# A transformer tower on one core: patch weights on four row groups, and the second item's first stages moved into the attention of the first

## Time and profile before

| | us |
|---|---|
| median of 3 runs | 4034.71 (4033.22 to 4037.4) |
| the profiled execution, its own time | 4041.78 |
| its span | 4040.0 |
| first score of the phase `first` starts | 120.93 |
| TensorE busy | 3811.9 (94%) |
| VectorE busy | 2886.2 (71%) |
| ScalarE busy | 2619.9 (65%) |
| GpSimd busy | 860.0 (21%) |

### The profile page before, as it was taken

One profiled execution on the slowest core, in us unless ns is written; L12 is line 12 of the kernel. 1 busy time (PEld: TensorE's weight loads), 2 busy tenths in 40 slices (PEclk: granted clock), 3 DMA queues, 4 the chain that ended last, 5 costly groups with the idle time before them and its releaser, 6 DMA issues.

```text
span 4040.0 us, 62363 instructions
## 1 busy us (share of the span) xinstructions
PE 3811.9 (94%) x21508; PEld 1330.2 (33%) x21508; DVE 2886.2 (71%) x4955; ACT 2619.9 (65%) x4768; POOL 860.0 (21%) x1263
## 2 busy tenths in 40 slices
PE   6988999999999999999999999999999999999896
PEld 3223333333333333333333333333333333333232
DVE  3866767778686777867678676777867677777672
ACT  0555767667676666767667676666767667676564
POOL 4122113122121322213122121312213122121211
PEclk7899999999999999999999999999999999999998
DMA  5203211222012122111222122122111222111100
GB/s 106 40 15 60 43 36 33 46 48 44 22 35 56 33 43 43 37 34 33 46 48 43 27 38 49 32 43 47 38 29 33 50 44 43 31 36 25 28 6 6
DMA packets 119067, 156.36 MB, mean 39 GB/s; under 512 B 24847, under 2 KB 66575, under 8 KB 118717
## 3 DMA queue, kind: packets, MB, share of 16 engines
q1 hardware_dynamic: 118753, 152.38, 19.0%
HBM read 120.01 MB, written 29.36 MB: 37 GB/s over the span
## 4 chain that ended last, share of the span: by engine, by line
PE 81%; ACT 8%; issue 4%; DVE 3%; SPq 2%; DMA 1%; POOL 1%; ACTq 0%; POOLq 0%; DVEq 0%
PE acc L911 23%; PE side_st L897 21%; PE nat L885 19%; PE side_st L854 3%; PE side_st L750 3%; PE side_st L727 2%; ACT prob L1101 2%; PE side_st L840 2%; ACT hidden L1073 2%; PE side_st L807 1%; DVE tile_max L1294 1%; ACT hidden L1019 1%; PE side_st L772 1%; SPq L525 1%; PE side_st L765 1%
## 5 line engine op out<-in xcount | busy, mean ns | idle before, releaser
L1294 DVE TENSOR_REDUCE tile_max<-nat 128x1 f32<-128x512 f32 x4096 | 2585.7, 684 | 1002.6 <-PE nat L885 972.0
L1101 ACT ACTIVATE prob<-side_st 128x512 f32<-128x512 f32 x4096 | 2205.8, 600 | 1271.7 <-PE side_st L897 1236.8
L897 PE MATMUL side_st<-q_rows,k_rows 99*128 99x512 bf16 x4096 | 1562.6, 384 | 45.9 <-ACT prob L1101 28.9
L885 PE MATMUL nat<-k_rows,q_rows 96*128 96x512 bf16 x4096 | 1532.2, 385 | 30.2 <-DVE tile_max L1294 24.0
L911 PE MATMUL acc<-prob,v_padded 128*32 128x512 f32 x8192 | 1096.1, 607 | 14.5 <-ACT prob L1101 13.5
L897 PEld LDWEIGHTS side_st<-q_rows,k_rows 99*128 99x128 bf16 x4096 | 398.6, 98 | 1213.9 <-ACT prob L1101 812.1
L885 PEld LDWEIGHTS nat<-k_rows,q_rows 96*128 96x128 bf16 x4096 | 400.8, 98 | 508.4 <-DVE tile_max L1294 276.1
L1455 POOL TENSOR_SCALAR max_parts<-neg_max 128x16 bf16<-128x16 f32 x128 | 26.5, 207 | 1868.4 <-DVE neg_max L1301 1868.3
L911 PEld LDWEIGHTS acc<-prob,v_padded 128*32 128x32 f32 x8192 | 162.3, 108 | 377.4 <-ACT prob L1101 216.0
L840 PE MATMUL side_st<-ln_rows,w 64*128 64x512 f32 x512 | 139.5, 622 | 28.7 <-ACT hidden L1073 23.2
L1380 POOL TENSOR_SCALAR ln_s<-ln_s 128x8 f32<-128x8 f32 x64 | 13.0, 203 | 676.8 <-DVE ln_s L1202 673.2
(11 more groups left out here) (124 smaller groups left out, 1994.5 us busy)
## 6 DMA issues: line engine op xcount, KB each, us to landing
q_rows<-q_scratch SPq DMA_DIRECT2D x576, 64.0 KB
k_rows<-k_scratch SPq DMA_DIRECT2D x192, 192.0 KB
x_rows<-in_x SPq DMA_DIRECT2D x62, 512.0 KB, 6.3
q_scratch<-hidden SPq DMA_DIRECT2D x32, 384.0 KB
k_scratch<-hidden SPq DMA_DIRECT2D x96, 128.0 KB
group_weights<-in_routed SPq DMA_DIRECT2D x64, 129.0 KB, 2.1
q_rows<-max_rows SPq DMA_DIRECT2D x512, 3.0 KB
out_h<-out_rows SPq DMA_DIRECT2D x16, 256.0 KB, 2.1
```

What stands on the lines that cost most here:

```text
L885: eng.matmul(NAT[use % len(NAT)][:, :], QA[u][0:K_NAT, h, c:c + P], KA[u][0:K_NAT, h, kh * 512:kh * 512 + 512], start=True, stop=True)\
L897: eng.matmul(RING[TILE_BANK[n0 + n]][:, :], KA[u][0:K_ALL, h, t * P:t * P + P], QA[u][0:K_ALL, h, half * 512:half * 512 + 512], start=True ...
L1101: eng.activation(prob[:, n % TILES, :], RING[TILE_BANK[n0 + n]][:, :], ACT.Exp).then_inc(exp_done, 1)
L1294: eng.tensor_reduce(mx[:, q % 2, j // 8, j % 8 // 2, j % 2:j % 2 + 1], NAT[use % len(NAT)][:, :], AX.X, ALU.max).then_inc(nat_free, 1)
```

## The change

The table `dft` is now loaded four times, to partitions 0, 32, 64 and 96, by DMAs that ScalarE issues. W is loaded in four quarters of 72 KB by SP to the same four places (`w_rows`), all in `prob`. The 128 products go round the four row groups, and each row group writes to its own PSUM bank. VectorE makes 16 copies of 64 elements a partition in place of 8 of 128. `TOKB`, `TOKC`, `LN1` and `LN2` of item 1 leave the serial list and go to tiles 2, 6, 9 and 15 of `first`. `TR`, `QK`, `QV`, `VC`, `SCR` and `RL` of item 1 move from tiles 2, 5, 9, 13, 14 and 26 to 27, 31, 36, 39, 42 and 50. The load of the second half of item 1's x comes behind item 0's `RL` in the list.

```diff
--- before.py
+++ after.py
@@ -210,11 +210,12 @@
 
 
     start = [("TOKA", 0), ("TOKB", 0), ("TOKC", 0), ("LN1", 0, "0"), ("LN2", 0, "0"), ("TR", 0, "0"),
-             ("QK", 0, 0), ("QV", 0, 0), ("LX", 1, 0), ("TOKA", 1), ("SCR", 0, 0), ("VC", 0, 0), ("LX", 1, 1),
-             ("RL", 0, 0), ("HO0", 0), ("TOKB", 1), ("TOKC", 1), ("LN1", 1, "0"), ("LN2", 1, "0")]
+             ("QK", 0, 0), ("QV", 0, 0), ("LX", 1, 0), ("TOKA", 1), ("SCR", 0, 0), ("VC", 0, 0),
+             ("RL", 0, 0), ("LX", 1, 1), ("HO0", 0)]
     first = {n: [] for n in range(ATTN)}
-    for n, *stages in ((2, ("TR", 1, "0")), (5, ("QK", 1, 0)), (9, ("QV", 1, 0)),
-                       (13, ("VC", 1, 0)), (14, ("SCR", 1, 0)), (26, ("RL", 1, 0)), (56, ("WCL", 0)),
+    for n, *stages in ((2, ("TOKB", 1)), (6, ("TOKC", 1)), (9, ("LN1", 1, "0")), (15, ("LN2", 1, "0")),
+                       (27, ("TR", 1, "0")), (31, ("QK", 1, 0)), (36, ("QV", 1, 0)),
+                       (39, ("VC", 1, 0)), (42, ("SCR", 1, 0)), (50, ("RL", 1, 0)), (56, ("WCL", 0)),
                        (80, ("WCA", 0))):
         for k, part in enumerate(side_parts(stages)):
             first[n + (1 if part[0] == "RL" else 2) * k].append(part)
@@ -395,7 +396,7 @@
 
         CT = sb("const", [P, P + 200])
         ident = CT[:, 0:P]
-        w_low = prob[0:18, 4:8, :].rearrange("p (a b) c -> p a (b c)", a=2)
+        w_rows = prob[:, 4:6, :].rearrange("p b c -> p (b c)")
         low, upp = CT[:, P:P + 64], CT[:, P + 64:P + 128]
         fold = CT[:, P + 128:P + 192]
         half_pow = CT[:, P + 192:P + 200]
@@ -419,7 +420,7 @@
         W1 = sb("w_1", [P, E, HID])
         W2 = sb("w_2", [P, E, 64])
         B2 = sb("b_2", [P, 64])
-        dftc = sb("dft", [18, 16])
+        dftc = sb("dft", [P, 16])
         T3 = sb("bias_table", [WINDOW, WINDOW])
         routes = sb("routes", [1, B * G], I32)
         scr = [nc.dram_tensor(f"q_scratch{a}", (PARTS, 64, N_TOK), BF16, kind="Internal").ap()
@@ -537,10 +538,8 @@
                         eng.dma_start(xe[64 * hh:64 * hh + 64, :], item[:, T - 1, :]).then_inc(edge_in, 16)
 
 
-            load(dftc[:, :], dft, s_dft)
-
-            load(w_low, w_dft[:, 0:32].rearrange("f (a o) c -> f a (o c)", a=2), s_dft)
-            load(HE[0:18, 0:2, :], w_dft[:, 32:64].rearrange("f (a o) c -> f a (o c)", a=2), s_dft)
+            for r in range(4):
+                load(w_rows[32 * r:32 * r + 18, :], w_dft[:, 16 * r:16 * r + 16].rearrange("f o c -> f (o c)"), s_dft)
             load_x(0, 0)
             load_x(0, 1)
             twice = (slice(0, 64), slice(64, P))
@@ -682,15 +681,17 @@
         def _(eng):
             reg = [None]
             at = counter(reg)
-            eng.wait_ge(s_dft, 48)
-
-            for part, w in enumerate((w_low, HE[0:18, 0:2, :])):
-                wv = w.rearrange("f a (o c) -> f a o c", c=64)
-                for o in range(32):
-                    for c in (0, 64):
-                        mm = eng.matmul(SIDE[part][c:c + 64, o * 16:o * 16 + 16], wv[:, o // 16, o % 16, :],
-                                        dftc[:, :], start=(o == 0), stop=True, skip_group_check=True)
-                mm.then_inc(s_pe, 1)
+            eng.wait_ge(s_dft, 128)
+
+            wv = w_rows.rearrange("f (o c) -> f o c", c=64)
+            for o in range(16):
+                for c in (0, 64):
+                    for r in range(4):
+                        rows = slice(32 * r, 32 * r + 18)
+                        mm = eng.matmul(four[c:c + 64, 512 * r + o * 16:512 * r + o * 16 + 16], wv[rows, o, :],
+                                        dftc[rows, :], start=(o == 0), stop=True, skip_group_check=True)
+                        if (o, c) == (15, 64):
+                            mm.then_inc(s_pe, 1)
 
             eng.wait_ge(s_dma, N_SET[s_dma])
             for a in range(2):
@@ -961,6 +962,8 @@
         def _(eng):
             reg = [None]
             at = counter(reg)
+            for r in range(4):
+                eng.dma_start(dftc[32 * r:32 * r + 18, :], dft).then_inc(s_dft, 16)
             eng.wait_ge(s_dma, N_SET[s_dma])
 
             def full(n, k, use=0):
@@ -1128,18 +1131,18 @@
                 ins = eng.memset(tile[64:K_ALL, :, :], 0.0)
             step(ins)
             step(eng.memset(KA[0][K_MAX:K_ALL, :, :], 1.0))
-            eng.wait_ge(s_pe, 2)
-            for part in range(2):
-                for hh in range(2):
-                    src = SIDE[part][64 * hh:64 * hh + 64, :].rearrange("c (o a p) -> c a o p", a=2, p=8)
-                    for a in range(2):
-                        ins = eng.tensor_copy(
-                            Wf[64 * hh:64 * hh + 64, :, a, 32 * part:32 * part + 32].rearrange("c j o -> c o j"),
-                            src[:, a, :, 4 * hh:4 * hh + 4])
+            eng.wait_ge(s_pe, 4)
+            by_group = four.rearrange("c (r x) -> c r x", r=4)[:, :, 0:256].rearrange("c r (o a p) -> c a r o p", a=2, p=8)
+            for hh in range(2):
+                half = slice(64 * hh, 64 * hh + 64)
+                for a in range(2):
+                    for j in range(4):
+                        ins = eng.tensor_copy(Wf[half, j, a, :].rearrange("c (r o) -> c r o", r=4),
+                                              by_group[half, a, :, :, 4 * hh + j])
             step(ins)
             eng.wait_ge(s_dma, N_SET[s_dma])
             step(eng.tensor_copy(hot, prob[0:2 * WINDOW, 0:2, :].rearrange("p a c -> p (a c)")))
-            eng.wait_ge(s_pe, 4)
+            eng.wait_ge(s_pe, 6)
             for a in range(2):
                 ins = eng.tensor_copy(bias_f[:, a * 512:a * 512 + 512], NAT[a][0:WINDOW, :])
             step(ins)
```

## The result

The changed kernel takes 4049.05 us (median of 7 runs, 4045.86 to 4055.07), the kernel before 4034.71 (7 runs, 4033.22 to 4037.81). The ratio is 1.0033, with a 95% interval of 1.0022 to 1.0044: 13.3 us slower (8.9 to 17.8). On another chip, later, it was 1.0026 (1.0016 to 1.0036; 9 runs against 13), or 10.5 us. The forecast was 4041.1, the range 4032 to 4047: the time lies 2 us above its upper end. I had held no change beyond 0.2% likeliest; it is 0.33% slower, and the whole interval lies above 1.

The account below looks back on a forecast made before the run. TensorE bounds the main loop and `first`; the start is bound by loads, then SP's DMA issues. Terms −0.3 + 0 + 5.8 + 1.6 − 0.7 = +6.4 us on the median 4034.71 gave 4041.1; range 4032 to 4047.

Parts of the forecast that it names:

- two credits: In `first`: QK at the high clock, −1.0 us, and the clock rising some 2 us earlier, −1.5 us.
- the last step: Scaling: profiled execution stood 7.07 us over the median, so +6.4 was added to 4034.71, giving 4041.1 instead of 4048.2.
- patch weights: At the kernel's start: some 10 us of matmuls go, nearly all becoming waiting for loads; −0.3 us, bounds −3 and +1.8.
- start of the scores, the rest: Before item 1's phase: SP's issuing decides the first score, at about 121.0 against 120.93; 0 us, bounds −1.7 and +2.8.
- TOKB and TOKC: Item 1's stages moved into `first`, where TensorE is the bound: 6.2 and 2.0 us more.
- QK: In `first`, at tile 31: runs at the high clock, 2.08 us becoming 1.04; −1.0 us.
- TensorE's waits: In `first`: ScalarE's copies +0.5 us, LN2 delaying TN +1.6, the max-row wait at tile 64 going −0.7.
- earlier rise of the clock: In `first`: TOKB's dense work lifts TensorE's clock some 2 us earlier, worth −1.5 us on tiles 2 to 7.
- Line 697 still starts near 20.3: Sign at the kernel's start: the bias products begin near 20.3 us although the patch-weight products are shorter.
- Rival 1: Before the first score: queue frees early, maxima decide, scores at 112; −8.9 us instead of 0, time 4032.2; chance 0.15.
- Rival 2: In `first`: item 1's reload comes late for tile 82; up to +4 us, 4045.1; chance 0.27 including other upper bounds.
- Rival 3: At the start: patch weights count in full, loads at 17.5, along with the early queue; −5.5 us or more; chance 0.06.

Follow-up runs that it names:

- r4_before: The kernel before, unedited, run and profiled once more beside the repeated changed kernel: 4033.9 us.
- r2_late: The changed kernel with the 43 late loads issued behind the first super tile's max rows, their wait moved to tile 30: 4040.01 us, ratio 1.0003.
- r2_tok: The changed kernel with item 1's TOKB and TOKC back in the serial list and x ahead of the reload: 4038.87 us, ratio 1.0002.

## Why the prediction was wrong

The mechanism was right in most: the saved matmuls became waiting, SP decided the start, the stages moved into `first` made the loss. The step that failed is the sum: two credits, −2.5 us, that only a late clock in the profiled execution gave, waits of +1.4 that measured 3.4 to 3.8, and the last step, which put that execution's difference on the median.

Its terms against the traces. The first row is the start of the bias products; that its 1.5 us reach the first score isn't shown, and "the rest" holds what they don't. The third column takes the change as I did, against the profile of before; the fourth against r4_before.

| term | predicted | against the profile I had | against r4_before |
|---|---|---|---|
| patch weights | −0.3 | −1.5 | −1.3 |
| start of the scores, the rest | 0 | −0.8 | +2.2 |
| TOKB and TOKC | +8.2 | +6.5 | +6.5 |
| QK | −1.0 | −0.95 | 0 |
| TR | −0.4 | −0.5 | −0.5 |
| TensorE's waits: ScalarE's copies +0.5, TN +1.6, max rows −0.7 | +1.4 | +3.4 | +3.8 |
| earlier rise of the clock (what is left) | −1.5 | −1.4 | +0.2 |
| sum, by the mark | +6.4 | +4.8 | +10.9 |

**Patch weights: right in kind.** I said that the matmuls' 10 us would become waiting for the `s_dma` loads. The loads did decide when the bias products start; ahead of them the timeline shows 7.2 us of "issue" and then 2.7 of waiting for the loads. Four at once was my lower bound for the products. "Line 697 still starts near 20.3" was 1.3 us out: before, TensorE was in fact not waiting for the loads at all. Its last 33 records ran from 18.67 and the bias products followed without a wait; the loads land about 19 (at 19.88 in the run of the patch weights alone). Two readings of mine were off: 256 records of 54 ns are 13.9 us and not 14.9 (with the gap of 0.8 it was 14.8), and the granted clock of that stretch is 1.00, so 1.2 GHz is not its clock. The Trainium skill, TensorEngine Tiling (Array Packing), section Instruction Overhead, gives each matmul an overhead of about 60 cycles. What I concluded from it, that four row groups would save little and this part be +1.8, did not hold in the timeline: the records came 3.7 times as fast and the bias products earlier, not later. The time cannot tell: the ratio of the patch weights alone, 0.9989 to 1.0006, holds +1.8 us too. The 15 ns of a record are 35 cycles at the granted clock, those of a product of two records 70 (an estimate from the 3.24 us); which of the two the 60 are to be held against, no run shows.

**The start of the scores: right, with the sizes near.** SP decided; the max rows were the last wait, at 118.61 to 120.45 against my 121. SP's late loads ended at 116.7 in the profile that I had, but at 112.6 to 114.7 in the other four of before; I gave them 113.7 after the change and they ended at 110.3 to 112.0. The reason was wrong in part: I took 3 us off SP's stalls "behind it", behind x, and the four long issues were 13.8 us after and 13.4 before. They only began earlier, as the reload began at 66.83 and not at 69.3. What I took as 0 is +0.6 on the means. The rule of the Trainium skill's DMA: Bandwidth & Descriptors, Queues, rings and completion order, that each engine takes descriptors in ring order, agrees with the landing of the max rows: 4.22 us with x ahead of them, 1.75 to 1.78 without. Rival 1 fell for the reason given against it, and r2_late shows what it would have been worth: with SP free, the scores start at 109.5.

**Stages moved into `first`: the right cause, and here the sum failed.** The run with the tokens back in the serial part shows that it is TOKB and TOKC which cost most. They were even cheaper than I had them (4.51 + 2.00 in place of 6.2 + 2.0), since the clock rose in the midst of TOKB; in the other six traces with it TOKB took 4.91 to 5.96. What failed is the step "QK at 31 runs at the high clock: 2.08 becomes 1.04, −1.0" with "should lift the clock some 2 us earlier than before, worth −1.5". Both credits are right in size against the trace that I read, but not against all executions of before: in two of its five traces QK already takes 1.13 us and the clock rises 3.7 and 3.9 us behind the first score, as early as with the change. These two are the ones whose time (4033.9 and 4031.94) lies within 3 us of the median; the other three took 4041.78 to 4043.92. Against the two the change has no credit of 2.5 us to take. That TOKB lifts the clock, the reason given for the −1.5, isn't shown by any run.

**The waits: undersized.** I allowed for ScalarE's copies and LN2 (+2.1), less 0.7 for a wait that should go. TensorE's waits grew by 3.4 to 3.8 us. LN2's share was right in kind and 1.0 in place of 1.6 (the split before had ended 1.1 us ahead of TN, not 1.3: 142.30 + 0.22 against 143.60). ScalarE's was larger: acc waits 1.2 us behind TOKB, as the copies (L984, L986 and L987, 125.54 to 126.84) stand between two exponentials. VectorE's copy and first sum, which I had at nothing ("lie beside TensorE"), held up `nat` for 0.7 us (to 134.43 and 136.22), as tile maxima stand behind them; in r2_tok, where the copy is out of the phase and the sums are not, this wait is gone. And "the last 0.65 us wait for max rows at tile 64 goes" did not hold: the wait went to tile 96 (0.73 us at 201.41, in the timeline above), where the max rows now come late.

**The scale: 7 us taken off whole.** "Against the profiled execution's own 4041.78 that is 4048.2; it stood 7.07 over the median, so on the scale of the median 4034.71 + 6.4 = 4041.1." This step takes a difference as if the 7 us that the profiled execution had too many lay outside the change. Its mark stands 3.4 us behind the mean of five traces of the same kernel, and 6.2 behind r4_before's, whose time is next to the median. These are us of the very stretch that the change rewrites, and that in the changed kernel come out nearly the same each time (the phase takes 108.4 to 108.8 us in three traces, against 98.5 to 102.3 before). Put plainly: I read the kernel before in an execution with a late clock in the phase, and took as the change's gain what the two traces near the median have without it. On the profiled execution's own scale the sum gave 4048.2, and the measured median is 4049.05; it was this step that took it to 4041.1. (That the two agree to 0.9 us is partly luck: by the mark the sum was 1.6 too high against that trace, and 2.5 of the difference lies behind the mark.) Against r4_before the start cost 10.9 us, 4.5 more than the sum. The medians of the result lie 14.3 us apart; the 3.4 that are left lie behind the mark or in the spread, and their cause stays open.

**Rivals 2 and 3.** Rival 2 had the right side and the wrong mechanism. Item 1's reload was not late: TensorE's waits of the phase hold none of `nat` for the reload. Rival 3 fell with the loads at 19. The chances: "slower" had 0.27, for a cause that did not occur and for the upper bounds together; it was the upper bounds. The range went only to rival 2 with one of these, 4047. Several small costs of one sign in a bound stage should have been let add up.

## What to carry to other kernels

Ask of a stage not how long it takes but who waits for it: 10 us of matmuls disappeared from a place where the next ones had to wait for loads all the same (1.5 us came of it there), and 6.5 us of matmuls and a layer norm put where TensorE is the bound brought 3 us of waits with them. Before a saving is read out of one profiled execution that lies above the median, find out where in it the excess lies; if it is in the stretch that the change rewrites, the credits taken there (a clock that rises earlier, a shorter stage) are not the usual execution's, and the difference may not be put on the median unchanged. Where many small DMAs stand on a queue's issuing engine ahead of one that is waited for, look at both its producer and its place. Here maxima that end some 11 us earlier brought the first score nothing as long as the late loads stood ahead of the max rows; with the maxima late, the loads' place had at most some 1.6 us to give (max rows copied at 115.2, SP free at 116.7 in the profile of before) and nothing in the run of the patch weights alone; the two together brought 9 to 10.

## What the runs showed of the hardware that was not expected

- Four row groups, each with its own PSUM bank, gave 3.7 times the rate on products of 18 x 64 by 18 x 16 in float32: 12.12 us for 223 records became 3.24 to 3.25, at a granted clock of 1.00 both times. So the 54 ns of a record are not a floor for each instruction. Whether the row group or the bank set them, no run shows.
- Behind these 223 records TensorE stood for 7.0 to 7.2 us for "issue", with nothing in the profile that it waits for, and then ran the last 33 in 0.66 us, at 15.6 to 16.1. Before, a gap of 0.60 to 1.20 us stands behind the same 223rd record, and the last 33 came at 18.41 to 18.96 in five traces. No run tested what it is. It cost nothing here, as the loads came later still, but it would limit faster patch weights.
- The kernel before varies in its first 220 us by 6 us from one execution to the next: 3.2 by the first score, with the end of SP's late loads (between 112.6 and 116.7), and 3.8 in the phase, longest where TensorE's granted clock rises latest (3.7 to 9.5 us behind the first score). The granted clock from 120 to 130 us is anything from 0.50 to 0.93 in the five traces, with the same instructions before it.
- Issues on SP that follow the reload (24 DMAs) and the one-hot rows (6) can take 2 to 4 us each in place of 0.3, whichever DMA it is: four small late loads, with or without x ahead of the reload (13.4 and 13.8 us), or x itself (8.62 us for two). What they wait for, no run shows.
